# Gated cross attention with routed experts: adds moved beside GpSimd's roots, the plan of the experts and one tile moved

## The reference

```
lat = layernorm(layernorm(x))
q = lat @ Wq.T
k, v = split(concat(layernorm(ctx) @ Wkv.T, lat @ Wlkv.T))
qn, kn = rmsnorm(q, qn_g) * SCALE, rmsnorm(k, kn_g)        # per head, 4 heads of 64
p = softmax(where(mask, qn @ kn.T, -max))
att = (p @ v) @ Wo.T + bo
x = x + tanh(g_xattn) * att
h = layernorm(x)
prob = softmax(h @ w_router); top 2 of 8 experts
y = x + tanh(g_ffn) * sum over the two of gate * (gelu(h @ w1[e] + b1[e]) @ w2[e] + b2[e])
```

## Time and profile before

| what | value |
|---|---|
| median of 3 runs | 905.99 us (902.59 to 906.76) |
| profiled execution, its own time | 906.47 us |
| span of its trace | 904.7 us |
| PE busy | 855.7 us (95%) |
| DVE busy | 645.3 us (71%) |
| ACT busy | 511.5 us (57%) |
| POOL busy | 289.5 us (32%) |
| chain that ended last, by engine | PE 56%, DVE 17%, issue 13%, POOL 8%, ACT 4% |

### The profile page before, as it was taken

The page is one execution under the profiler, slowest core; times in us unless marked ns, Lnnn a source line. Parts: engine busy times, 40 slices in busy tenths (PEclk is TensorE's granted clock), DMA queues, the critical chain, the costliest instruction groups (busy, mean ns, idle before and its releaser), DMA issues.

```text
span 904.7 us, 19559 instructions
## 1 busy us (share of the span) xinstructions
PE 855.7 (95%) x5968; PEld 657.3 (73%) x5968; DVE 645.3 (71%) x1500; ACT 511.5 (57%) x1371; POOL 289.5 (32%) x241
## 2 busy tenths in 40 slices
PE   3898999999999999999999999899999999999995
PEld 3654555545555455555469999899999999999995
DVE  6766777768777667676897777775755776676695
ACT  2668875787857877468841843443433443353462
POOL 2321212221265212641054238332332322232233
PEclk8899999999999999999999999999999999999998
DMA  4801000130012201120044649352442535362272
GB/s 128 248 1 50 1 1 1 47 96 1 7 54 82 94 1 56 50 94 1 2 137 99 181 82 259 58 144 47 96 90 43 137 72 114 47 145 45 37 230 27
DMA packets 71896, 70.26 MB, mean 78 GB/s; under 512 B 18593, under 2 KB 66977, under 8 KB 71841
## 3 DMA queue, kind: packets, MB, share of 16 engines
q1 hardware_dynamic: 57696, 52.73, 20.0%
q0 software_dynamic: 13152, 16.86, 10.9%
q10 hardware_dynamic: 992, 0.00, 0.1%
HBM read 44.04 MB, written 26.31 MB: 78 GB/s over the span
## 4 chain that ended last, share of the span: by engine, by line
PE 56%; DVE 17%; issue 13%; POOL 8%; ACT 4%; DMA 1%; another core or an unknown queue 0%; SPq 0%; POOLq 0%; DVEq 0%; ACTq 0%
PE psS L1705 22%; PE psF L1901 10%; PE psO L1901 10%; DVE p_sum L1141 6%; PE psS L1822 4%; POOL rr L681 4%; POOL routed L691 3%; PE psO L1838 3%; PE psF L1705 2%; PE psF L1869 1%; ACT sq L828 1%; DMA xr<-in_x 1%; PE psO L1850 1%; DVE Q L1124 1%; PE psO L1705 1%
## 5 line engine op out<-in xcount | busy, mean ns | idle before, releaser
L889 ACT ACTIVATE V<-psS,b_col 128x256 f32<-128x256 f32 x280 | 116.9, 470 | 214.8 <-PE psS L1705 195.3
L699 POOL DMA_INDIRECT out<-V,token_i x70 | 121.5, 1736 | 261.8 <-DVE V L1332 240.5
L872 ACT ACTIVATE p_ring<-psS,shift 128x1024 f32<-128x1024 f32 x128 | 136.6, 1111 | 71.7 <-PE psS L1822 69.7
L681 POOL TENSOR_TENSOR rr<-ssm,minus_half 128x4 f32<-128x4 f32 (+1 forms) x72 | 76.1, 1057 | 282.4 <-DVE ssm L1105 282.4
L1838 PE MATMUL psO<-p_ring,V 128*64 128x512 f32 x576 | 148.5, 612 | 0.0
L1141 DVE TENSOR_TENSOR p_sum<-p_sum,p_ring 128x1024 f32<-128x1024 f32 (+1 forms) x112 | 135.7, 1211 | 1.3
L1901 PE MATMUL psF<-ln_hi,K 128*128 128x256 f32 x560 | 124.2, 285 | 0.2
L1822 PEld LDWEIGHTS psS<-Q,K 64*128 64x128 f32 x864 | 77.0, 187 | 61.3 <-issue 41.9
L1822 PE MATMUL psS<-Q,K 64*128 64x512 f32 x864 | 121.3, 413 | 0.0
L1901 PE MATMUL psO<-ln_hi,K 128*128 128x256 f32 x560 | 120.5, 279 | 0.0
L1309 DVE CAST K<-V 128x512 fp32r<-128x512 f32 x140 | 60.4, 431 | 59.1 <-ACT V L889 57.0
(11 more groups left out here) (297 smaller groups left out, 1766.5 us busy)
## 6 DMA issues: line engine op xcount, KB each, us to landing
xr<-in_L_ffn_w SPq DMA_DIRECT2D x11, 1024.0 KB, 8.2
xn<-in_L_ffn_w SPq DMA_DIRECT2D x11, 1024.0 KB, 5.6
lnf<-routed SPq DMA_DIRECT2D x35, 258.0 KB
routed<-pad_rows SPq DMA_DIRECT2D x17, 258.0 KB, 9.9
xr<-in_x SPq DMA_DIRECT2D x8, 512.0 KB, 4.5
xb<-in_x SPq DMA_DIRECT2D x4, 1024.0 KB, 6.1
out<-xb SPq DMA_DIRECT2D x4, 1024.0 KB
b_raw<-in_L_ffn_b SPq DMA_DIRECT2D x11, 128.0 KB, 3.5
```

What stands on the lines that cost most here:

```text
L681: pool.tensor_tensor(rr[0:p, c % 2, n], ssm[0:p, c % 2, n], minus_half[0:p, n], ALU.pow).then_inc(rr_ready, 1)
L699: pool.indirect_dma_start(out_rows, bass.IndirectOffsetOnAxis(ap=token_i[:, m:m + 1], axis=0), y_out[:, m, :], None, bounds_check=NTOK - 1 ...
L872: act.activation(p_ring[0:p, u % RING, :], psS[u % 2][0:p].rearrange("p a n -> p (a n)"), ACT.Exp, bias=bias).then_inc(exp_done, 1)
L889: act.activation(g32[:, q % 2, (c % 2) * TM:(c % 2 + 1) * TM], psH[q][:, (c % 2) * TM:(c % 2 + 1) * TM], ACT.Gelu_apprx_tanh, bias=b1_col[ ...
```

## The change

Five edits:

1. DVE: in groups other than i = 0 (and other than i = 5 of even windows, and a group in which router_logits stands there) the add of unit 2g-2 moves from ahead of heads_lo to behind mean_squares, that is between ssm and qkd. These are 43 adds.
2. DVE: norm_offsets for sequence 1 moves from group 5 of window 0 to group 4.
3. DVE: plan_experts moves in tile 7 from ahead of move_meta to behind keep_expert, beside plan_switches.
4. PE: in all odd windows, no longer in window 7 alone, the sums of the first half stand behind the scores of group 6 in place of the end of group 5.
5. PE: tile 5 of the experts is written out, and the loop starts at 6.

```diff
@@ -1465,7 +1465,10 @@
                     waited = past and i < 2 if even else more and i in (1, 3)
                     if waited:
                         heads_lo(turned_at(g))
-                    if g >= 1:
+                    summed = summed_at(g) is not None
+                    routed_here = not even and past and not last and i == 3
+                    between = tile_at(g) is not None and g >= 1 and i != 0 and (i != 5 or (w % 2 == 1 and w + 1 < WINDOWS)) and not routed_here
+                    if g >= 1 and not between:
                         add_probabilities(2 * g - 2)
                     if not even and past and last and i == 2:
                         router_logits(b - 1)
@@ -1480,9 +1483,10 @@
                         heads_lo(turned_at(g))
                     if tile_at(g) is not None:
                         mean_squares(tile_at(g))
-                    if not even and past and not last and i == 3:
+                    if between:
+                        add_probabilities(2 * g - 2)
+                    if routed_here:
                         router_logits(b - 1)
-                    summed = summed_at(g) is not None
                     if g >= 1 and not ahead and summed:
                         add_probabilities(2 * g - 1)
@@ -1496,7 +1500,7 @@
-                    if even and more and b == 0 and i == 5:
+                    if even and more and b == 0 and i == 4:
                         norm_offsets(b + 1)
@@ -1630,8 +1634,6 @@
                         activate(t, q)
-                    if t == 7:
-                        plan_experts()
                     move_meta(t)
@@ -1646,6 +1648,7 @@
                         if t == 7:
+                            plan_experts()
                             plan_switches()
                         results(t)
@@ -1933,6 +1936,7 @@
                     if w + 1 == WINDOWS and i == 6:
                         ranks(b - 1)
+                    if w % 2 == 1 and i == 6:
                         sums(2 * g - 4)
@@ -1946,7 +1950,7 @@
                         for u in (2 * g - 2, 2 * g - 1):
-                            if not folded:
+                            if not (w % 2 == 1 and i == 5):
                                 sums(u)
@@ -1986,7 +1990,12 @@
-                with pe.Fori(5, SURE - 1) as t:
+                for t in range(5, 6):
+                    first_layer(t)
+                    turn_tile(t + 1)
+                    second_layer(t)
+
+                with pe.Fori(6, SURE - 1) as t:
                     first_layer(t)
```

## The result

The changed kernel takes 908.42 us (median of 15 runs, 905.76 to 910.22), the kernel before beside it 903.97 us (15 runs, 902.04 to 906.76). The ratio is 1.0038, with a 95% interval of 1.0026 to 1.005: by the ratio some 3.4 us slower (the two medians are 4.5 us apart), which is more than nothing but less than the 0.5% that I had set as the bound of a difference. The profiled execution has a span of 906.9 us against 904.7.

A forecast was written before the change was run, and what follows sets the result against it. TensorE sets the time in attention and experts, so only its idle time can be given back; 906.5 + 4.7 (attention) - 1.6 (plan_experts moved) = 909.6 us. The forecast's own range was 902 to 914, the overall range 895 to 915 us.

The forecast's parts named there:

- the hold: Between ssm and qkd: an add beside GpSimd's rr stretches rr from 1.04 to 2.06 us, putting 1.03 us on the gap.
- R2: Rival: outside the opening groups the add does not delay rr, so TensorE's waits shrink; 895.5 us, chance 0.15.
- R4: Rival: an add behind rr's start waits for rr; same 2.3 us gap, so counted with the forecast, no chance of its own.
- Attention +4.7 us: Attention stage: window 1 +1.0, windows 2, 4 and 6 +2.1, windows 3 and 5 +1.6 us together; ends -3.1 and +7.3.
- Edit 4 gives nothing there: Window 1: the sums did not wait before, so moving them gains nothing, the same 1.08 us of sums in another place.
- takes this away: Windows 3 and 5: the sums' 0.71 us wait goes, since the next group's scores now stand ahead of them.
- Window 0 ... taken as nothing: Window 0: group 2's later qkd against sequence 1's earlier norm_offsets, net 0, ends -0.9 and 0.9 us.
- Case (a): Attention groups where VectorE itself is late: add of 1.13 us leaves, 1.03 us come in, 0.1 to 0.2 us gained.
- Edit 3, -1.6 us: End of tile 7: moving plan_experts behind removes TensorE's 1.56 us wait for w_lo; -1.6 us, ends -1.6 and 0.
- R1: Rival: tile 7's issue stall of 5.9 us goes once tile 5 is written out; 903.7 us, chance 0.25.
- R3: Rival: groups where VectorE waited for ScalarE ahead of ssm are the rule, tile 7's stall comes twice or longer; 915.5 us, 0.15.

## Why the prediction was right, and which of its steps were not

The forecast was 909.6 us against a profiled execution of 906.5, a move of +3.1 us; measured is a ratio of 1.0038, +3.4 us. The mechanism that carries the forecast, the hold, is shown by the runs. That the number came so near is in part luck: in the traces the attention cost 0.8 us more than in the sum and the experts gave 1.2 us more, and on a chip where the experts give nothing the move is larger (edits 1, 2 and 4 alone: a ratio of 1.0066). By its steps:

- **The hold, 0.9 us, as the rows of the six opening groups had it:** right, in size and in number (49 long rr). R2, that the add would not hold rr, did not happen (its price was 0.2 us off as well: 7.6 and 2 are 9.6 us, not 9.4). R4 held that an add behind rr's start would wait for rr; with rr 0.3 us ahead it waited in none of 35 groups.
- **Attention +4.7 us:** measured +5.5 and +5.1. Window 1 took +1.2 (foreseen 1.0), windows 2, 4 and 6 +0.5 each (0.7), windows 3 and 5 +1.0 each (0.8), window 0 +0.1 (0). Window 7 had nothing in my sum and took +0.85: its first sums (431.37) wait 0.62 us, behind adds of window 6's end that come later (in the kernel with the add first in 21 groups, which leaves the last of them in its place, window 7 takes +0.02 us). I had stopped where the moved adds stopped.
- **"Edit 4 gives nothing there" (window 1) and "takes this away" (0.71 us in windows 3 and 5):** this step failed. I priced edit 4 by the waits that stood in the trace of before, not by those that edit 1 would make. With edit 1 in, the sums' wait without edit 4 is 1.51 and 2.15 us, and edit 4 is worth 1.5 to 1.6 us in each of three windows. Nor does it take all of the wait away: in windows 3 and 5 the sums still wait 0.56 and 0.57 us, where I had named no wait as the sign of being right.
- **"Window 0 ... taken as nothing":** the net is right (+0.1 us), but as a difference of terms beyond the ends of 0.9 us that I gave: without edit 2 the turn of group 7 waits 2.32 us. Of these 1.42 us stood in the trace of before, and my sum did not count them. Edit 1 by itself costs 14.4 us, edits 2 and 4 give 8.9 us of it back.
- **Case (a), 0.1 to 0.2 us gained where VectorE is late:** wrong. The 21 groups, all but one of this kind, cost as much in sum as all 43.
- **Edit 3, -1.6 us:** the wait for w_lo at the end of tile 7 went, as said; tile 7 is 3.2 us shorter. But the wait was only 0.92 us in the second trace of before and 0.68 us with edits 3 and 5 undone. On the chips where the slow issue is short the two tiles take 27 us with edits 3 and 5 and 26 to 27 us without them, so it isn't 1.6 us of each run.
- **R1, the stall goes with the peel:** no. Tile 7 is still 16.1 us, with slow issue at a second pass of the loop instead of a third; in the kernel with GpSimd first it falls in tile 8 (15.61 us) and tile 7 takes 11.64 us. R3 did not happen.

## What to carry to other kernels

An idle time of one engine that waits for another may be no free room if both read SBUF: look first for a place in the trace where the two already stand side by side, and in which order. If the order matters, let the engine whose result is awaited start first by a short instruction. Here the attention was 7.5 us longer with the add first in 43 groups, and some 4 to 5 us shorter with the root first in 21 or 13 chosen groups, both against the kernel with edit 1 undone; with the root first in 35 of the 43, it was 7 us longer. And price the edits of one change in the state that the others make: a wait that isn't in the trace of before may be the one that an edit is there to remove.

## What the runs showed of the hardware

- A VectorE add with both inputs in SBUF that starts first delays GpSimd's root until 0.86 to 0.91 us behind the add's end, in all 49 places of the change (rr 1.91 to 2.06 us instead of 1.01 to 1.04). With GpSimd first by 0.3 us both run at their own length in 35 of 35 places (rr 1.01 to 1.04, add 1.20 to 1.22 us). With GpSimd first by 0.02 to 0.04 us they do in 19 of 20 places in one trace and 11 of 12 in another; in the one left in each, rr takes 2.11 us. The Trainium skill (page "SBUF — State Buffer", section "Who interferes with whom") calls the lock exclusive, and for the two-port modes it says that whoever issues first has it for the whole instruction while the other blocks fully. The measurement decides: this holds for the add first (rr 1.92 us), and not for this small root first (add 1.20 us beside rr). An explanation would be that GpSimd reads its few elements at the start of the microsecond that the root takes; that is argued and not shown.
- A product of one SBUF input (1024 columns in 0.69 us) holds it in the same way (rr 1.39 us, 0.86 us behind the product's end).
- Tiles 7 and 8 of the kernel before take 3.7 us or 7.7 us more than two plain tiles (11.85 and 11.64 us), in its two traces, which are from different chips; slow issue and the wait for w_lo are both in it.
